# A reordered second prelude, routing and seams, with fewer identity turns, in a one-core decoder layer

## The reference, cut to what matters

```python
x1 = layernorm(x + retention(x))            # 16 heads, decay masks, group norm, silu gate
x2 = layernorm(x1 + ssm(ctx_1024, z=x1))    # in_proj, 4-tap conv, silu, softplus step,
                                            # scan over 256 steps and 16 states, * silu(z)
p  = softmax(x2 @ Wg.T); top 2 of 8 experts # routing
y  = layernorm(x2 + ffn(x2, p))             # W1, W3, W2 shared; low-rank A/B pairs by expert
```

## Time and profile before

| what | value |
|---|---|
| median of 3 runs | 434.84 us (433.22 to 438.58) |
| profiled execution | 437.9 us, of it span 436.1 us |
| mean granted clock | 0.937 |
| PE busy | 373.7 us (86%) |
| DVE busy | 306.3 us (70%) |
| POOL busy | 217.6 us (50%) |
| ACT busy | 185.8 us (43%) |
| chain that ended last | PE 48%, DVE 24%, issue 11%, ACT 7%, POOL 7% |

### The profile page before, as it was taken

How to read it: one execution, slowest core, us unless ns; L and a number is a source line. 1 busy time by engine, 2 the same in 40 slices (tenths; PEclk the granted TensorE clock), 3 DMA queues, 4 the chain that set the end, 5 groups by cost and what they waited for, 6 DMA issues and landing times.

```text
span 436.1 us, 7090 instructions
## 1 busy us (share of the span) xinstructions
PE 373.7 (86%) x2524; PEld 322.7 (74%) x2524; DVE 306.3 (70%) x631; ACT 185.8 (43%) x444; POOL 217.6 (50%) x223
## 2 busy tenths in 40 slices
PE   3847769679798785999989799998989999999993
PEld 2635657557667775999777698977879898899982
DVE  6386997774679698698567999855799965552223
ACT  2593435434236764352266555226556421331111
POOL 6056794967428658364046665404666631242030
PEclk9988998688779989799999999998989999999998
DMA  6492441012012133120110331021042200000000
GB/s 206 158 349 95 163 177 26 24 30 82 0 36 48 54 115 89 58 66 0 42 70 17 120 111 61 2 73 45 7 123 96 74 0 2 2 24 2 2 0 24
DMA packets 13490, 29.12 MB, mean 67 GB/s; under 512 B 1928, under 2 KB 3216, under 8 KB 13200
## 3 DMA queue, kind: packets, MB, share of 16 engines
q1 hardware_dynamic: 11584, 25.27, 17.4%
q10 hardware_dynamic: 1872, 3.41, 2.6%
HBM read 27.49 MB, written 1.18 MB: 66 GB/s over the span
## 4 chain that ended last, share of the span: by engine, by line
PE 48%; DVE 24%; issue 11%; ACT 7%; POOL 7%; DMA 1%; SPq 1%; DVEq 0%; POOLq 0%; ACTq 0%
PE xf L1060 21%; PE a2p L1060 10%; PE gen L1060 7%; PE ret L1060 5%; DVE gen L1590 4%; PE acc L1060 4%; DVE ret L1590 3%; DVE ring L1656 2%; DVE sc L1607 2%; POOL wsplit L579 2%; DVE ring L1598 2%; DVE fth L1835 2%; DMA wattn_sb<-in_wattn 1%; ACT L789 1%; POOL x L616 1%
## 5 line engine op out<-in xcount | busy, mean ns | idle before, releaser
L1060 PE MATMUL xf<-am,wsplit 128*128 128x256 f32 x672 | 96.0, 294 | 0.4
L1060 PEld LDWEIGHTS xf<-am,wsplit 128*128 128x128 f32 x672 | 87.6, 195 | 2.5 <-DVE work L1846 1.5
L572 POOL TENSOR_TENSOR ring<-decay,brow 128x512 f32<-128x512 f32 x48 | 60.7, 1282 | 17.6 <-PE acc L1060 17.2
L683 POOL TENSOR_TENSOR work<-work,ratioT 128x256 f32<-128x256 f32 x28 | 21.7, 774 | 92.3 <-DVE work L1846 85.1
L1060 PE MATMUL a2p<-work,wff_sb 128*128 128x256 f32 x224 | 57.7, 380 | 0.5 <-POOL work L683 0.5
L1835 DVE SCALAR_TENSOR_TENSOR fth<-fth,xf 128x256 f32<-128x256 f32 x56 | 23.3, 415 | 45.0 <-ACT fth L1000 44.8
L1000 ACT ACTIVATE fth<-xf 128x256 f32<-128x256 f32 x56 | 21.0, 375 | 77.0 <-PE xf L1060 75.1
L1060 PE MATMUL xf<-x2s,wsplit 128*128 128x256 f32 x336 | 50.3, 301 | 0.2
L1060 PE MATMUL acc<-ident,ring 128*128 128x128 f32 x256 | 37.6, 282 | 12.8 <-DVE ring L1598 9.8
L1060 PEld LDWEIGHTS acc<-ident,ring 128*128 128x128 f32 x256 | 30.2, 144 | 21.6 <-DVE ring L1598 12.5
L1060 PEld LDWEIGHTS xf<-x2s,wsplit 128*128 128x128 f32 x336 | 44.6, 196 | 1.8 <-DVE work L1846 0.7
(11 more groups left out here) (314 smaller groups left out, 762.2 us busy)
## 6 DMA issues: line engine op xcount, KB each, us to landing
brow<-bc_dram SPq DMA_DIRECT2D x26, 256.0 KB, 3.5
crow<-bc_dram SPq DMA_DIRECT2D x24, 256.0 KB, 3.3
work<-in_wsp SPq DMA_DIRECT2D x3, 896.0 KB, 9.0
wff_sb<-in_wff SPq DMA_DIRECT2D x2, 896.0 KB, 8.5
am<-bc_dram SPq DMA_DIRECT2D x1, 1536.0 KB, 9.9
brow<-bc_dram ACTq DMA_DIRECT2D x6, 256.0 KB, 4.0
wattn_sb<-in_wattn SPq DMA_DIRECT2D x1, 1280.0 KB, 5.5
xT_sb<-in_xT SPq DMA_DIRECT2D x4, 256.0 KB, 4.1
```

What stands on the lines that cost most here:

```text
L572: pool.tensor_tensor(ring[:, i % RING], du_of(b)[:, j].unsqueeze(1).broadcast_to([P, UN, S]), brow[:, c % 2], ALU.mult).then_inc(sem["driv ...
L683: pool.tensor_tensor(xs[:, n % 4], fq[:, m % 2], ratioT[:], ALU.mult).then_inc(sem["xs_ready"], 1)
L1060: return pe.matmul(o, l, r, skip_group_check=True, **kw)
```

## The change

It writes the lists anew from slot 10 to the start of stage 1 and in the seams.

- Second prelude: `context(1)` moves from slot 11 to 10, `conv_input(1)` and `conv_tanh(1)` from 12 to 11, `conv(1)` from 12 to 11, `conv_gate(1)` from 13 to 12, `low_rank(1)` from 13 to 12, `step_size(1)` from 14 to 12, `softplus_exp(1)` from 14 to 12 and `softplus_log(1)` from 14 to 13, `step_small(1)` and `step_sum(1)` from 15 to 13.
- Routing of batch 0: `logits` directly behind `flip_x2`, `route` part 1 from slot 12 to 11, `A1` and `A3` to the front of slot 12. Slots are masked in order 0, 1, 2, 3 instead of 0, 2, 1, 3.
- Batch 3's first group-norm steps, batch 2's norm shift and POOL's roots move partly into stage 1; POOL makes drives 0 and 1 before its lows; `attended(B - 1)` moves to the front of step 4.
- Seams: ACT copies `MK` and `MD` before the logarithm and then touches Exp once; `decays` 0 moves ahead of the last `am_high`; DVE's order of masks, step sum and lows changes.
- Identity turns: 12 ahead of `values(1, 0)` stay; `flip_x2(0)` has 6; `logits(0)` gets 8; those of `low_rank(1)` and `start_y(1)` go.
- Banks and their waits follow the new order.

```diff
@@ gen_order
         if i == 11:
-            uses += [("X2", 0)]
+            uses += [("X2", 0), ("LG", 0)]
+        if i == 12:
+            uses += [("A1", 0), ("A3", 0)]
...
-        uses += {9: [("Z", 0)], 11: [("LG", 0), ("IN", 1)], 12: [("A1", 0), ("RT", 0), ("A3", 0), ("MK", 0), ("MD", 0)],
-                 13: [("DBL", 1)], 14: [("DT", 1), ("RW", 0)]}.get(i, [])
+        uses += {9: [("Z", 0)], 10: [("IN", 1)], 14: [("RW", 0)],
+                 12: [("DBL", 1), ("RT", 0), ("MK", 0), ("MD", 0), ("DT", 1)]}.get(i, [])
@@ pool, first
-                    if i == 14:
-                        second_masks(b)
                     if i == 15:
                         inputs(nb)
                         drive_unit(nb, 0)
                         drive_unit(nb, 1)
+                        second_low(b, 1)
+                        root(s - 2, ve1, rs1, "r1_ready", 7, "r1_pow")
             def stage(b, fb, nb):
+                if fb == 0:
+                    second_low(fb, 3)
+                    second_sum(fb)
...
+                    if n == 0 and fb == 0:
+                        root(B - 1, gvar, grs, "gn_step", 9, "gn_pow")
@@ act, first
                     if i == 11:
                         turned(b)
                         rounded(b)
+                        act.wait_ge(sem["w_low"], 2 * PER_W)
+                        conv_input(nb)
                         weighed(b)
+                        conv_tanh(nb)
                     if i == 12:
-                        act.wait_ge(sem["w_low"], 3 * PER_W)
-                        conv_input(nb)
+                        low_rank(nb)
                         routed(b)
-                        conv_tanh(nb)
                         spread(b)
+                        softplus_exp(nb)
                     if i == 13:
-                        am_high(b, (0, 1))
-                        low_rank(nb)
-                        am_high(b, (2, 3))
-                    if i == 14:
-                        softplus_exp(nb)
+                        split_high(2, 3)
+                        am_high(b, (0, 1, 2))
                         softplus_log(nb)
+                        am_high(b, (3,))
                     if i == 15:
                         ratios(b)
+                        start_y(nb)
                         decays(nb, 0)
-                        start_y(nb)
                         decays(nb, 1)
@@ act, seam
                     softplus_exp(nb)
-                    softplus_log(nb)
                 if b is not None:
                     spread(b)
-                    am_high(b, (0, 1))
+                if nb is not None:
+                    softplus_log(nb)
+                    act.activation(exp_at[:], mhalf[:], ACT.Exp).then_inc(sem["act_const"], 1)
+                if b is not None:
+                    am_high(b, (0, 1, 2))
+                if nb is not None:
+                    decays(nb, 0)
+                if b is not None:
+                    am_high(b, (3,))
                 if nb is not None:
                     start_y(nb)
...
@@ pe
             def low_rank(b):
-                if b == 1:
-                    stay_awake(g[:, 0, 0:P], 12)
             def start_y(b, fb):
+                need(pe, "y_init", b, 2)
                 if fb is not None:
-                    need(pe, "am_ready", fb, 3)
-                if b == 1:
-                    stay_awake(acc[:, 0, 0:P], 12)
-                need(pe, "y_init", b, 2)
+                    need(pe, *emptied(("RW" if fb == 0 else "A1", fb)))
@@ pe, first
                     if i == 11:
                         flip_x2(b)
+                        logits(b)
+                    if i == 12:
+                        expert_inputs(b, "A1", A1)
+                        expert_inputs(b, "A3", A3)
...
-                    if i == 11:
-                        logits(b)
+                    if i == 10:
                         context(nb)
                     if i == 12:
-                        expert_inputs(b, "A1", A1)
+                        low_rank(nb)
                         route_rows(b)
-                        expert_inputs(b, "A3", A3)
                         spread_rows(b, "MK", 0)
                         spread_rows(b, "MD", 1)
-                    if i == 13:
-                        low_rank(nb)
+                        step_size(nb)
                     if i == 14:
-                        step_size(nb)
                         spread_rows(b, "RW", 2)
                         base(b, 1)
@@ pe, flip_x2 and logits
-                    stay_awake(g[:, 0, 0:P], 12)
+                    stay_awake(g[:, 0, 0:P], 6)
...
+                if b == 0:
+                    stay_awake(g[:, 0:P], 8)
@@ dve, first
+                    if i == 12:
+                        conv_gate(nb)
+                    if i == 15:
+                        group_mean(s - 1)
...
+                    if i == 11:
+                        second_part(b)
+                        route(b, 0)
...
+                    if i == 11:
+                        conv(nb)
+                        route(b, 1)
...
                     if i == 13:
-                        conv_gate(nb)
-                        masked_inputs(b, (0, 1))
-                        masked_inputs(b, (2, 3))
+                        masked_inputs(b, (0, 1, 2, 3))
+                        group_stats(B - 1)
+                        step_small(nb)
                         input_lows(b)
-                    if i == 15:
-                        step_small(nb)
                         step_sum(nb)
@@ dve, stage
+                    if n == 4 and fb == 0:
+                        attended(B - 1)
...
                 if nb is not None:
                     step_small(nb)
+                if b is not None:
+                    masked_inputs(b, (0, 1))
+                if nb is not None:
                     step_sum(nb)
                 if b is not None:
-                    masked_inputs(b, (0, 1))
+                    masked_inputs(b, (2, 3))
                 second_input(fb, 1)
```

More of the change, by code:

```diff
@@ L616, in gated, with second_low, second_sum @@
                 pool.tensor_tensor(x1[:, s], x1[:, s], gate[:], ALU.mult).then_inc(sem["ro_ready"], 1)
-            def second_masks(b):
+            def second_low(b, slot):
+                need(pool, "amh_ready", b, slot + 1)
+                need(pool, "aml_ready", b, 2)
+                pool.tensor_tensor(am[:, 1, slot], am_full[:, slot], am[:, 0, slot], ALU.subtract
+                                   ).then_inc(sem["aml_pool"], 1)
+            def second_sum(b):
                 need(pool, "am_ready", b, 4)
                 mkT = mkTs[b % 2]
-                for i in (2, 3):
-                    need(pool, "amh_ready", b, i + 1)
-                    slot = AM_ORDER[i]
-                    pool.tensor_tensor(am[:, 1, slot], am_full[:, slot], am[:, 0, slot], ALU.subtract
-                                       ).then_inc(sem["aml_pool"], 1)
                 pool.tensor_tensor(mkT[:, 1], mkT[:, 0], mkT[:, 1], ALU.add).then_inc(sem["mk1_ready"], 1)
@@ L643, in first @@
                         decayed_queries(s)
-                    if r == 1 and s > 1:
+                    if r == 1 and 1 < s < B:
                         root(s - 2, ve1, rs1, "r1_ready", 7, "r1_pow")
-                    if r == 2 and 0 < s <= B:
+                    if r == 2 and 0 < s < B:
                         root(s - 1, gvar, grs, "gn_step", 9, "gn_pow")
@@ L1616, in masked_inputs @@
                     need(dve, "kd_ready", B - 1, 1)
-                for i in which:
-                    slot = AM_ORDER[i]
+                for slot in which:
                     half = slot // 2
@@ L1625, in input_lows @@
             def input_lows(b):
-                for i in range(2):
-                    need(dve, "amh_ready", b, i + 1)
-                    slot = AM_ORDER[i]
+                for slot in (0, 2):
+                    need(dve, "amh_ready", b, slot + 1)
                     dve.tensor_tensor(am[:, 1, slot], am_full[:, slot], am[:, 0, slot], ALU.subtract
@@ L1814, in stage @@
             def stage(b, fb, nb):
-                if fb > 0:
-                    end_sum(fb - 1)
                 for n in range(len(MAIN)):
                     units = SCANS[n] if b is not None else []
+                    if n == 0 and fb > 0:
+                        end_sum(fb - 1)
+                    if n == 4 and fb == 0:
+                        attended(B - 1)
                     if nb is not None and n == 11:
@@ L1851, in stage @@
                         norm_stats(fb - 1, r3, st3, mv3, ve3, "r3_ready", 2)
+                    if n == 0 and fb == 0:
+                        norm_shift(B - 2, mv1, rs1, nm1, "r1_pow", "r1_shift")
                     if n == 1:
@@ L1857, in stage @@
                         group_scale(B - 1)
-                    if n == 4 and fb == 0:
-                        attended(B - 1)
                     if n == 5 and fb == 0:
```

46 lines of the change are left out of this document (19 added, 27 removed).

## The result

The changed kernel takes 431.04 us (median of 12 runs, 427.89 to 431.51) against 434.50 (12 runs, 433.07 to 438.58): the ratio of the runs is 0.991, 95% interval 0.988 to 0.993. It is faster by 3.5 us, about 0.9%, where the forecast's terms took off 12.6. Of the 12 runs two lie at 427.9, the other ten near 431; the profiled one is one of the two (427.92 us, span 425.8), while the profiled execution of before (437.9) lies 3.4 above its median. All ratios leave out a kernel's runs that lie over 1.5% above its fastest, which here touches `best_again` alone.

The account below looks back on a forecast made before the run. Stage 1's front was taken to hold about 10 us of waiting, with PE waits and slow clock in the prelude. 437.9 - 4.5 + 0.9 - 6.7 - 2.3 = 425.3 profiled, 422.2 us median; range 416 to 431.

Parts of the forecast that it names:

- Front of stage 1: First `hidden` to context projection of stage 1: 35.2 us instead of 41.9, minus 6.7; bounds 31.8 and 39.
- rival 1: POOL becomes the bound in stage 1's front: scans 2 to 7 wait, front 39, total 427 us; chance 0.14.
- rival 3: Slower: PE's clock at the lower level throughout stage 1's front, 57 us instead of 35.2, total 444; chance 0.06.
- First `hidden` and first scan: Second prelude into stage 1: `hidden` 4.5 us earlier, less 0.9 for the clock; first scan 7.9 us earlier, at 142.8.
- 8.0 us of the 8.7 remain: Second prelude: the chain starts 8.7 us earlier at `conv_input(1)`, and POOL's `inputs` still starts 8.0 us earlier.
- new idle time of 2.5 us ... I take 0.9: PE waits 2.5 us between `group_var(2)`'s bank wait and release; slow clock behind it was priced at 0.9 us.
- upper bound of 4.5: All 9 us of PE work behind the new idle time at the lower clock, half hidden: plus 4.5 us.
- rival 2: Prelude gain fails to arrive: DVE's conv and routing delay score products, PE's wait grows to 5; 430 us, chance 0.12.
- Identity turns: Prelude: 48 become 26; upper clock level expected through 124.9, no separate gain counted.
- Seams: Seams 1 and 2: PE and scan starts gain 2 x 0.3 + 1.2 + 0.5 = 2.3 us; bounds 0 and 4.8.
- 2 x 0.3 on PE: Seams: PE's 1.19 us wait before `MD` goes, but `end_sum`'s sum is late by some 0.9: 0.3 gained per seam.
- The base: Start of the sum: profiled execution of before, 437.9 us, taken as 3.1 above the median of the runs shown.

Follow-up runs that it names:

- best_again: The same kernel as splits_turns, run once more: median 428.9 us over 6 runs, ratio 0.978 to before.
- the controls: The kernel before and the changed kernel, both unchanged, each profiled a second time: 435.9 and 431.5 us (one run each).
- att_only: The kernel before with only `attended(B - 1)` moved to the front of DVE's step 4 of stage 1: 433.1 us, ratio 0.997.
- ctl_before: The kernel before, unchanged, for a second profile: 435.9 us (one run).
- splits_early: The changed kernel with ACT's last three weight-block roundings moved to slot 11 and POOL's low halves to slot 12: 431.2 us, ratio 0.990.
- splits_guard: splits_early with POOL also waiting for DVE's group scale before the weight blocks: 428.6 us, ratio 0.983.
- turns_scores: The changed kernel with 12 more identity turns on PE ahead of batch 3's score products: 427.4 us, ratio 0.986.
- splits_turns: splits_guard plus the 12 identity turns of turns_scores: 423.8 us (4 runs), ratio 0.975.
- route_late: The changed kernel with DVE's second routing part of batch 0 moved behind slot 12's score products and the group variance: 430.8 us, ratio 0.990.
- log_first: The changed kernel with ACT's seam logarithm back ahead of the `MK` and `MD` copies, early Exp touch kept: 429.7 us, ratio 0.990.
- order_after: The changed kernel with two more POOL waits: inputs for `gdev`'s squares, first second-mask low for `gate_silu(3)`: 430.2 us, ratio 0.989.
- order_best: splits_turns with the two more POOL waits of order_after: 428.0 us, ratio 0.985.
- no_turns: The changed kernel without the 6 identity turns ahead of `flip_x2` and the 8 ahead of `logits`: 431.1 us, ratio 0.989.

## Why the prediction was wrong

Between the controls the three terms of the sum miss by 5.6 us (v to hidden), 2.3 (front) and 0.6 (seams): 8.5 of the 12.6 forecast did not come, 4.1 did.

1. **Front of stage 1: right in length.** 35.6 and 35.8 us measured, 35.2 forecast. POOL did not stretch it to rival 1's 39, and rival 3's front at the lower level did not come (PEclk 0.87 and 0.95; in the first trace the first `hidden` itself is slow, 5.47 for 3.11). att_only gives 2.9 of the controls' 4.4 us; the rest wasn't taken apart. The size of the gain was too large by 2 us: before's profiled 41.9 is at a lower mean clock (0.88) than ctl_before's 40.2 (0.92), and I subtracted from it.

2. **First `hidden` and first scan: the step that failed.** I had v to hidden fall by 3.6 (4.5 less 0.9); between the controls it rose by 2.0. The scan was to come 7.9 us sooner by "8.0 us of the 8.7 remain"; it came 0.8 sooner in one pair and 0.5 later in the other. The chain does start early: from v, `step_size` comes 9 to 10 us sooner than before (v + 28.5 and 28.2, was 38.7 and 36.9). But the forecast had it at v + 25.8 (127.7 in the frame of before's trace), and the gap grows from there: `chunk_state` is 3.1 to 3.4 us later than forecast, the first `hidden` 4.4 to 4.8 (against a forecast that has the 0.9 in it), the first scan 6.9 to 7.2. Two terms of the walk fail. First, "new idle time of 2.5 us ... I take 0.9": it was 3.07, and PE ran at the lower level until about 133 in the first trace. My own upper bound of 4.5 was nearer to the 3.1 to 3.4. The row that I cited for it (2.1 busy of 4.8, then slow) pointed the right way by luck: in ctl_before the same stretch, 2.1 busy of 4.8, is followed by work at the upper level. Second, DVE's part was priced with durations of single rows, except the lows; in the new order `step_small` takes 2.78 us instead of the 1.08 of splits_early, `gdev` 1.25 instead of 0.16, `gate_silu` 1.80 instead of 0.68, each beside a POOL instruction. The runs price them: POOL's part alone 2.0 us of v to end (splits_guard), the clock's part 0.6 to 0.9 (turns_scores), both 4.3 (splits_turns) when the clock stayed up, and 2.0 to 2.3 when it did not (best_again). That the two together give more than the sum has one reason that shows: turns_scores does not hold the clock (0.67 behind `chunk_state`), and its two lows take 3.18 instead of 2.24. Another I only argue: while PE is slow DVE waits for `chunk_state`, which hides part of what POOL costs DVE, and the reverse.

   This is rival 2's place and in part its course ("one in-order queue passes the delay on"), and the time is near its 430. Its wait of 5 us did not come, and route_late, which takes the routing part out of that queue's way, gained nothing. I gave it 0.12 "because it needs two things together". They aren't independent here: all seven traces with the wait of 3.07 or 3.08 have the lower level behind it.

3. **Identity turns: half right.** The clock is 1.00 from 111 to 120, as forecast, but ctl_before has it so with the old turns; the change isn't shown to have brought it. And "taking them away saves nothing by itself" hid the other side: without the 14 that stay, the trace is 1.5 to 1.8 us longer up to the context projection.

4. **Seams: right in mechanism, 0.6 short in size.** Between the controls they gave 1.7 of the 2.3: 0.6 in stage 2 (I had 1.2) and 1.0 in stage 3 and behind (I had 0.5). In both stages PE's first wait for a scan (0.39) goes; in stage 3 one of 1.26 becomes 0.91. log_first keeps these gains, so they don't come from the exchange of logarithm and copies; which of the other seam edits (the early Exp touch, decay 0 ahead of the last `am_high`, DVE's order) brings them wasn't tested apart. The 2 x 0.3 on PE did not come: the 1.19 returns as 0.92 before `end_sum`, which I had named as what is late next. The figure that I weighed against this, about 2.66 us for each change of table with load and drain (the Trainium skill, ScalarE: Activation LUTs, "What ACT_TABLE_LOAD costs"), finds no support in the trace: the load at 216.56 takes 1.28 and the exponential follows 0.01 behind it.

5. **The base.** The forecast went from one profiled execution (437.9) and took off 3.1 for the median. That execution is longer than ctl_before's at three places (front 1.6, half stage with the second seam 1.7, v to hidden 1.3), at a lower mean clock (0.937 against 0.947). The slow stretch from 113.80, which I took for a property of the kernel, is absent in ctl_before and att_only. Part of my gains was the removal of such things, which the median doesn't contain. Between the profiled executions 10.0 us went; between the medians 3.5.

## What to carry to other kernels

When a chain is pulled ahead on in-order queues, walk every queue that it now crosses to the point where the next stage starts; a chain that begins some 9 us sooner can end where it was, because the work that it overtakes is late instead. Price a DVE operation with two inputs in SBUF by the POOL instruction that may be running beside it, not by its own length, however small it is, and look at who then waits: in the traces here a wait added to POOL paid off once (splits_guard) and cost more than it gave twice (order_after, order_best). Take gains from parts of a trace that repeat in a second execution, and compare positions from a mark that the change leaves alone. splits_turns is the version to keep of those tried, with a caution: by the medians of all runs it is at 0.974 and 0.987 of before in its two sets, the change at 0.992, and it isn't shown that its turns add to what splits_guard has (0.985).

## What the hardware did that I had not expected

DVE waits for whole POOL instructions. `gdev` began at 141.77 and ended at 143.02, within 0.01 of the end of POOL's `inputs`; in order_best `gate_silu` missed the meeting of two drives by 0.02 us and took 1.1 more than its 0.68. The Trainium skill, SBUF — State Buffer, "Who interferes with whom", says it: a DVE instruction with two SBUF inputs and a GpSimd instruction that reads SBUF exclude each other for the whole instruction, whichever came first. These runs agree; the scans, which have one of their inputs in PSUM, stay at 1.22 beside POOL's work. An operation with a single input in SBUF was stretched too: the first of `step_small` took 1.27 us where splits_early has 0.39.

The clock behind a wait is not a function of the wait. Behind 3.07 us ahead of the variance product it fell in every trace that has this wait (PEclk 0.55 in the window shown above); behind 2.82 at the same product in ctl_before only the next eight matmuls were long. Behind 1.63 ahead of batch 3's projection it fell in before and stayed up in ctl_before and att_only. Behind the same 1.62 it stayed up in splits_turns and order_best and fell in best_again; behind 2.0 ahead of the context projection it was down in att_only and no_turns and up in six others; behind 1.19 in a seam it fell in att_only and stayed up in log_first. In the first 15 us it differs from execution to execution as well, and v with it, from 98.9 to 103.7. What sets it in one execution and not in another stays open.
